# A graph layer with experts on one core: the hand-over from the edge loop to the node tiles

## The reference, cut to what matters

```python
edge_index = jnp.stack([src, dst])
xn = _layernorm(x, axis=-1)
x = x + _L0_gnn_ref(xn, edge_attr_3, ..., edge_index) + _L0_mix_ref(xn[None], ...)[0]
x = x + _L0_ffn_ref(_layernorm(x, axis=-1)[None], ...)[0]

# inside _L0_gnn_ref
agg = jax.ops.segment_sum(msgs, dst, num_segments=atom_feature.shape[0])
return atom_feature + agg

# inside _L0_ffn_ref
gate_logits = xf @ Wg + bg
top_w, top_i = jax.lax.top_k(gate_logits, TOP_K)
top_w = jax.nn.softmax(top_w, axis=-1)
```

## Time and profile before

| | us |
|---|---|
| median of 3 runs | 1286.27 |
| lowest and highest | 1279.44, 1294.23 |
| the profiled execution, its time | 1295.63 |
| its span | 1293.7 |
| TensorE busy in it | 1114.3 (86%) |
| VectorE, ScalarE, GpSimd busy | 770.7, 626.2, 657.7 |

### The profile page before, as it was taken

One profiled execution on the slowest core, in us unless ns is written; L12 is line 12 of the kernel. 1 busy time (PEld: TensorE's weight loads), 2 busy tenths in 40 slices (PEclk: granted clock), 3 DMA queues, 4 the chain that ended last, 5 costly groups with the idle time before them and its releaser, 6 DMA issues.

```text
span 1293.7 us, 26994 instructions
## 1 busy us (share of the span) xinstructions
PE 1114.3 (86%) x8025; PEld 1052.4 (81%) x8026; DVE 770.7 (60%) x1946; ACT 626.2 (48%) x1945; POOL 657.7 (51%) x726
## 2 busy tenths in 40 slices
PE   1457888888898988889888889879999999999996
PEld 1447878888898888788788889659999999999995
DVE  6957767677777777777777856582333333333331
ACT  3238434344444444444444457515656565656552
POOL 2762665656566566566666413072454454444442
PEclk9578988889889888989898999889999999999998
DMA  8331322323222322232322203437522222222221
GB/s 215 101 93 38 91 82 78 91 83 89 85 87 84 89 85 85 81 89 84 86 82 82 63 2 101 134 140 284 163 41 40 33 36 36 36 36 32 41 33 21
DMA packets 46321, 105.19 MB, mean 81 GB/s; under 512 B 13637, under 2 KB 24438, under 8 KB 44102
## 3 DMA queue, kind: packets, MB, share of 16 engines
q0 software_dynamic: 30720, 69.24, 21.5%
q1 hardware_dynamic: 15558, 35.42, 8.6%
HBM read 87.68 MB, written 16.94 MB: 81 GB/s over the span
## 4 chain that ended last, share of the span: by engine, by line
PE 77%; issue 7%; DVE 6%; ACT 3%; another core or an unknown queue 2%; DMA 1%; POOL 1%; SPq 1%; DVEq 1%; POOLq 0%; ACTq 0%
PE ps L855 21%; PE ps L1020 16%; PE ps L1034 15%; PE ps L783 8%; PE ps L768 4%; PE ps L832 4%; PE ps L815 2%; PE ps L906 1%; PE ps L902 1%; ACT e L1175 1%; PE ps L1004 1%; DMA attr_raw<-in_edge_attr 1%; PE ps L931 1%; POOL free_hot L632 1%
## 5 line engine op out<-in xcount | busy, mean ns | idle before, releaser
L563 POOL DMA_INDIRECT xg<-xn_rows,idx_st x416 | 422.4, 1015 | 302.3 <-issue 107.0
L855 PE MATMUL ps<-sel,xg 128*128 128x120 f32 x2496 | 327.9, 287 | 26.2 <-issue 25.4
L855 PEld LDWEIGHTS ps<-sel,xg 128*128 128x128 f32 x2496 | 314.0, 204 | 32.5 <-issue 31.6
L1020 PEld LDWEIGHTS ps<-xst,w_st 128*128 128x128 f32 x1792 | 211.0, 194 | 5.0 <-issue 2.2
L1020 PE MATMUL ps<-xst,w_st 128*128 128x128 f32 x1792 | 211.5, 277 | 1.7 <-ACT ht_sb L1331 1.1
L1331 ACT ACTIVATE ht_sb<-ps,b_cur 128x128 f32<-128x128 f32 x448 | 127.8, 368 | 168.2 <-PE ps L1020 168.2
L1034 PE MATMUL ps<-w_sb,ht_sb 128*128 x896 | 202.8, 379 | 0.8 <-DVE y_sb L1906 0.8
L668 POOL DMA_INDIRECT out<-y_sb,put_st x56 | 107.5, 1919 | 166.5 <-DVE y_sb L1909 144.2
L1034 PEld LDWEIGHTS ps<-w_sb,ht_sb 128*128 128x128 f32 x896 | 166.4, 191 | 21.4 <-issue 1.2
L783 PE MATMUL ps<-w_f,zt 128*128 128x128 f32 x832 | 133.0, 299 | 32.1 <-issue 31.9
L1175 ACT ACTIVATE e<-ps,neg_top 128x65 f32<-128x65 f32 x416 | 125.7, 326 | 54.3 <-DVE neg_top L1509 45.6
(11 more groups left out here) (294 smaller groups left out, 1445.6 us busy)
## 6 DMA issues: line engine op xcount, KB each, us to landing
w_sb<-in_L_ffn_W SPq DMA_DIRECT2D x16, 1024.0 KB
xg<-xn_rows,idx_st POOLq DMA_INDIRECT x416
x_sb<-in_x SPq DMA_DIRECT2D x5, 560.0 KB
xn_rows<-xn_sb SPq DMA_DIRECT2D x5, 560.0 KB
xn_t<-xn_rows SPq DMA_DIRECT2D x25, 112.0 KB
expert_in_rows<-xf_sb SPq DMA_DIRECT2D x12, 224.0 KB
out<-x_sb SPq DMA_DIRECT2D x12, 224.0 KB
b_bc<-in_L_ffn_b SPq DMA_DIRECT2D x1, 1024.0 KB, 4.5
```

The costliest lines, as they stand in the source:

```text
L563: pool.indirect_dma_start(xg[:, s, tt, M:M + D], None, xn_dram, bass.IndirectOffsetOnAxis(ap=idx_st[:, s, tt:tt + 1], axis=0)).then_inc(ma ...
L855: mm = pe.matmul(ps3[:, s, col:col + n], xg[:, r, tt, lhs0:lhs0 + 128], sel[:, s, lo:lo + n], start=(tt == 0), stop=(tt == TG - 1))
L1020: mm = pe.matmul(h_of(c), w1_st[:, s, kc, c, :], xst[:, s, kc, :], start=(kc == 0), stop=(kc == 1))
```

## The change

It has five parts, all in the hand-over and the node tiles except the last.

1. TensorE multiplies `ident` by `ones` twelve times (128 columns, into `ps1`) ahead of `gather_up(0)`; nobody reads the result.
2. The first chunk is staged by three engines: VectorE copies slots 1 to 3, ScalarE the upper half of slot 5 and then slot 0, GpSimd the lower half (slot 4). TensorE waits for two more semaphores there. The gate's padded weights `wg_pad` are made after the third chunk's staging and not before the first.
3. VectorE reads the `far` flag before it waits for the last sum, and not after.
4. From c = NC - 2 = 11 on, VectorE's list has `scales(c)` ahead of `choose(c - 2)`.
5. `stay_awake` is called with 1 and 4 in place of 3 and 5.

```diff
@@ GpSimd
-                for q0, slot in ((0, 4), (64, 5)):
+                for q0, slot in ((0, 4), (64, 5))[0:1 if c == 0 else 2]:
...
-            pool.wait_ge(staged_rest, 2 * NC)
+            pool.wait_ge(staged_rest, 2 * NC - 1)
@@ TensorE
-                pe.wait_ge(staged_rest, 2 * c + 2)
+                pe.wait_ge(staged_rest, 2 * c + 1)
+                if c == 0:
+                    pe.wait_ge(first_dve, 1)
+                    pe.wait_ge(first_act, 1)
...
+            for k in range(12):
+                pe.matmul(ps1[:, 0, 0:128], ident[:, :], ones[:, :], start=True, stop=True)
             gather_up(0)
             gather_up(1)
...
-            stay_awake(3)
+            stay_awake(1)
...
-            stay_awake(5)
+            stay_awake(4)
@@ ScalarE
             act.wait_ge(agg_final, 1)
-            act.wait_ge(gate_loaded, 32)
-            act.activation(wg_pad[:, :, :].rearrange("p c e -> p (c e)"), zero[:, 0:1].to_broadcast([128, 192]), ACT.Copy).then_inc(act_own, 1)
-            act.wait_ge(act_own, 1)
-            act.activation(wg_pad[:, :, 0:NE], wg_sb[:, :, :], ACT.Copy).then_inc(wg_padded, 1)
...
-            for c in range(3):
+            tiles = CHUNKS[0]
+            act.activation(agg_st[64:128, 0, 4, 0:len(tiles), :], agg[64:128, 5, 0:N].rearrange("q (p j) -> q j p", j=J)
+                           [:, tiles[0]:tiles[-1] + 1, :], ACT.Copy).then_inc(first_act, 1)
+            act.activation(agg_st[:, 0, 0, 0:len(tiles), :], agg[:, 0, 0:N].rearrange("q (p j) -> q j p", j=J)
+                           [:, tiles[0]:tiles[-1] + 1, :], ACT.Copy).then_inc(staged_wide, 1)
+            for c in (1, 2):
                 stage(c)
+
+            act.wait_ge(gate_loaded, 32)
+            act.activation(wg_pad[:, :, :].rearrange("p c e -> p (c e)"), zero[:, 0:1].to_broadcast([128, 192]), ACT.Copy).then_inc(act_own, 1)
+            act.wait_ge(act_own, 1)
+            act.activation(wg_pad[:, :, 0:NE], wg_sb[:, :, :], ACT.Copy).then_inc(wg_padded, 1)
@@ VectorE
+            far = dve.value_load(spread_i[0:1, 0:1], min_val=0, max_val=1)
             dve.wait_ge(main.added, G)
             dve.wait_ge(mix_added, 1 + J)
-
-
-            far = dve.value_load(spread_i[0:1, 0:1], min_val=0, max_val=1)
...
             dve.tensor_scalar(agg[:, :, N:NW], agg[:, :, N:NW], 0.0, None, ALU.mult).then_inc(agg_final, 1)
+            tiles = CHUNKS[0]
+            dve.tensor_copy(agg_st[:, 0, 1:4, 0:len(tiles), :], agg[:, 1:4, 0:N].rearrange("q s (p j) -> q s j p", j=J)
+                            [:, :, tiles[0]:tiles[-1] + 1, :]).then_inc(first_dve, 1)
...
             for c in range(NC + 2):
                 sums(c)
-                choose(c - 2)
-                scales(c)
+                if c < NC - 2:
+                    choose(c - 2)
+                    scales(c)
+                else:
+                    scales(c)
+                    choose(c - 2)
```

More of the change, by code:

```diff
@@ L343, in gps_layer_kernel @@
         staged_wide, staged_rest = sem("staged_wide"), sem("staged_rest")
+        first_dve, first_act = sem("first_dve"), sem("first_act")
         wg_padded, pairs_numbered = sem("wg_padded"), sem("pairs_numbered")
```

## The result

Over 20 runs of each kernel the median went from 1285.59 to 1275.39 us; the ratio, which is not the quotient of these two medians, is 0.9914 with a 95% interval of 0.9894 to 0.9934, which is 8.5 to 13.6 us less. The ratio leaves out one run of the changed kernel, the longest (1288.22 us), as a slow one. The profiled execution of the changed kernel took 1277.23 us, span 1275.3, 18.4 us less than that of the kernel before. Not all of this is the change: `agg_final` comes 9.3 us sooner (759.16 against 768.45), of which the flag explains a third of a microsecond; the rest lies in an edge loop whose instructions are the same.

The account below looks back on a forecast made before the run. Full-clock TensorE bounds the expert stage, so time saved ahead, where engines wait at hand-over, last chunks and totals, should pass through. 4.4 + 2.65 + 1.0 + 0.4 = 8.45 us off 1286.27 gives 1278 us, range 1267 to 1287.

Parts of the forecast that it names:

- The flag: Hand-over: loading the flag ahead of VectorE's wait for the last sum saves 0.4 us, between 0 and 0.8.
- The staging: First chunk: copies split over three engines, ScalarE last, let the first tile start about 1.5 us after `agg_final`.
- The clock at the first tiles: First chunks: twelve spare products keep TensorE at the full clock, removing 3.45 us of excess in chunks 0 and 1.
- The first term: Hand-over and first chunks together: flag, earlier staging and full clock give a lead that settles at 4.4 us.
- The last chunks: Last chunks: factors ahead of the choice let ScalarE's `normalise` start earlier, 2.65 us, with the half clock staying.
- The sums: Totals: one spare product in place of three removes VectorE's whole idle time there, 1.0 us.
- The rounds: Rounds of pairs behind the totals: 0.4 us gained, between -1.0 and 2.1, depending on the clock.
- Rival 1: First tiles: the clock falls in spite of the spares, costing the 3.45 us; 1281 us; chance 0.12.
- Rival 2: Full clock also in last chunks and rounds, flag gives 0.8: 10.25 us saved, 1276 us; chance 0.13.
- Rival 3: Expert loop: its shifted back edge brings a stall in each of 13 turns, 15.6 us; 1293.4 us; chance 0.05.
- Rival 4: Node tiles: ring of ScalarE and TensorE takes back the head start; 5.1 us saved, 1281 us; chance 0.08.

Follow-up runs that it names:

- spares alone: Kernel before plus only the twelve spare products ahead of the first tile; single execution 1148.65 us against 1144.61 for the kernel before.
- old staging: Changed kernel with first-chunk staging and `wg_pad` place as before, early flag and spares kept; `agg_final` to end 520.11 us against 516.12 for the change.
- all additions: Changed kernel plus new first-chunk split, spares at last chunks and ahead of experts, two at the sums, chunk 11's gate products earlier; 1281.69 us, ratio 0.9936.
- GpSimd held: Changed kernel with GpSimd's first staging copy waiting for VectorE's; `agg_final` to end 515.10 us against 516.12 for the change.
- first pair: First profiles of the kernel before and the changed kernel; last edge sum to end 526.78 against 517.34 us.
- second pair: Both kernels profiled again, unaltered, on another chip; last edge sum to end 529.50 against 517.27 us, medians 1287.12 and 1276.79, ratio 0.9912.
- spares ahead of experts: Changed kernel plus eight and four spare products around `place_spares` ahead of the first expert tile; `agg_final` to end 514.70 us against 516.12 for the change.
- no spares: Changed kernel without the twelve spare products ahead of the first tile; `agg_final` to end 519.00 us against 516.12 for the change.

## Why the prediction was right

Forecast 1278 us, 8.45 us less, in a range of 1267 to 1287; measured 1275.39, and 10.2 us less by medians. Its own steps:

**The flag: 0.4.** Measured 0.34 in both pairs (1.56 to 1.22). L1745 starts 0.93 us behind the last sum, forecast 0.85. Its price was about right and its part perhaps larger than foreseen: the same third of a microsecond takes TensorE's idle time from 2.02 to 1.68 us between "spares alone" and "old staging", and the clock fell in the one and held in the other, in one execution each.

**The staging: tile 0 at 1.5 us behind `agg_final`.** It was 1.74. ScalarE's two copies took 0.67 and 0.68 (forecast 0.74 each) and would have allowed 1.4; VectorE's took 1.57 where the step put 0.8 by a row of other form. So the step named the wrong engine as last. That explains 0.07 us; the first product starts 0.26 us behind VectorE's end, where in "all additions" and "GpSimd held" it starts 0.11 and 0.05 behind the last copy, and what fills the other 0.2 us the trace doesn't show. By the rule of the Trainium skill, "SBUF — State Buffer", in its part on the ports, VectorE's and GpSimd's copies would have followed each other. In the change they did not: both ran at once, and "GpSimd held" shows no waiting of the one for the other. In "all additions", where VectorE's copy is 500 elements in 0.68 us, GpSimd's copy beside it took 1.04 in place of 0.69. That goes the way of the lock that the page describes, but the 0.35 us more are less than the 0.53 for which the two ran side by side. Which copies take it, these two runs don't tell: the copies differ in size and in pace.

**The clock at the first tiles: 3.45.** It was 1.00 in all ten profiles that have both the spares and the early flag, nine of them with a split staging, and fell to half in the four others. No run has the split without the early flag. Chunk 0 took 2.84 us (760.91 to 763.75), forecast 2.82; chunk 3 began 10.99 us after `agg_final` (770.15), forecast 11.0, and waited for ScalarE's copy by 0.16 us, as written. The price held too: without spares chunk 2's products start 9.0 us behind the first tile and with them 5.7, which is 3.3 us, and 2.9 of it reach chunk 3, for which the change waits for ScalarE. One thing was off. The profile before was a mild case: in its repetition the half clock lasted to chunk 3, which came 2.6 us later still. That is the larger part of the gap between 9.4 us and 12.2 us in the two pairs. The first term as a whole, forecast 4.4, was 0.34 + 3.69 (20.06 to 16.37) = 4.0 in the first pair and 6.6 in the second.

**The last chunks: 2.65.** From chunk 3 to the last choice 47.50 became 44.63 us, 2.9; 3.4 in the second pair; 2.5 and 3.5 by the two runs that put the old order back, the 2.5 with the clock alike. That the half clock would stay was right for both profiles of the change and wrong for five other kernels with the same order, in which the last choice came 0.8 to 1.2 us sooner (two of the five have spare products there). Nothing that I tried decides which it will be. The sentence on "TensorE: Matmul & The Clock Gate", Part 4, of the Trainium skill (transposes don't count as busy) stays undecided with it: the transposes were the same in the runs with the full and with the half clock.

**The sums: 1.0.** Choice to totals 4.86 to 3.86 us, 1.0, and 5.88 to 3.86, 2.0, in the second pair. The mechanism was right, the term mis-sized as a constant: it depends on the clock. Three spares hold the totals by 1.0 to 2.0 us at the half clock and by nothing at the full one.

**The rounds: 0.4, between -1.0 and 2.1.** 26.20 to 25.42 us, 0.8, in the first pair, and 25.4 to 25.4, nothing, in the second. With the fall of "old staging" and "all additions" (28.05) it would have been -1.85, outside the bounds.

**The rivals.** Rival 1, the fall at the first tiles in spite of spares, did not happen in the change, which leaves 0.82 us of idle time behind the spares, but it did in "spares alone", with 2.02 us of it. Rival 2 happened in part: the second pair is its 10 us and more, by a clock that was lower before and not by one that was higher after. Rival 3 did not happen: from the experts' first written rows to the last it is 396.3 us in all fourteen profiles, whatever stood ahead of the loop. Rival 4 likewise: of 3.69 us won at chunk 3, none was given back at the choice. What I could not see from one execution was how much the kernel before varies; the measured 10.2 and 11.1 (by the ratio) lie 1.8 to 2.6 us over the sum. The mean of the two pairs puts that at 0.9 for the first term, 0.5 for the last chunks, 0.5 for the sums and 0.5 for the stretch from gather to end (426.61 to 425.84, 425.85 to 425.65), which I had at nothing. That last stretch varies by 1.8 us among kernels with the same expert code, so its 0.5 need not be the change's. That the sum came so near is in part luck: two of its terms hang on a clock that moves from one execution to the next, and they came out at 4.0 and 6.6, at 1.0 and 2.0.

## What to carry to other kernels

Spare products ahead of a wait are worth what the clock costs behind it (here 2.9 us), but look at the idle time that is left behind them: with 2.02 us of it they showed nothing here, with 1.68 and less they held the clock. So spares and what shortens the wait are to be tried together, since one of them alone may show nothing. Where three engines wait for each other in a ring, put the step that releases another engine's next work ahead of the step whose input comes late anyway. And size a term that rests on TensorE's clock from more than one execution of the kernel before.

## What was unexpected of the hardware

VectorE's copy with a stride of 25 took 1.57 us for 750 elements and 0.68 for 500, so its pace is not a constant of the engine: 2.1 ns an element in the copy of three slots and 1.4 in that of two. No run tells why.

The clock's falls move about between executions of the same instructions. Over the last gate products it was half in both profiles of the change and whole in "GpSimd held" and "spares ahead of experts".

The edge loop differs between chips by some 140 us, with instructions that are the same but for the place of the flag. Windows of 300 us, first the kernel before, then "no spares" on the other chip:

```profile
100.00:400.00 300.00, 257.91 (x1978) 246.38 (x1978) 221.47 (x561) 142.12 (x593) 172.28 (x173) 0.91 0.28 81
```

```profile
100.00:400.00 300.00, 298.63 (x2603) 293.33 (x2602) 282.25 (x727) 173.67 (x761) 224.47 (x226) 0.99 0.37 106
```

TensorE gets through 2603 records where it had 1978. On the slower one it stands in stalls of up to 1.2 us that no engine explains (31.1 us in 51 of them at one line, 20.9 in 37 at another, 17.3 in 30 at a third, in the changed kernel from 100 to 760 us), on the faster one in none that the list of waits shows, and the clock is 0.99 there and not 0.91. What causes the stalls was not tried and stays open; that it is the chip is likely, since each of the three chips of the experiments shows one kind of loop in all its profiles.
